# Decoder block with routed experts: the fourth round of token numbers moved ahead of the first expert

## The reference

```
logits = xf @ Wr + br                       # 2048 tokens, 8 experts
G, idx = top_k(softmax(logits).T, 256)      # each expert takes its 256 best tokens
tokens = xf[idx]
mid = silu(tokens @ W_up[expert // 2] + b_up)      # 256 -> 682
out = mid @ W_down[expert] + b_down                # 682 -> 256
y = zeros.at[idx].add(G * out)
```

## Time and profile before

| | us |
|---|---|
| median of 3 runs | 308.36 (307.84 to 310.17) |
| profiled execution | 308.39 |
| its span in the profile | 306.6 |
| busy: PE / PEld / DVE / ACT / POOL | 252.1 / 204.8 / 195.3 / 154.6 / 144.2 |

### The profile page before, as it was taken

One profiled execution on the slowest core, in us unless ns is written; L12 is line 12 of the kernel. 1 busy time (PEld: TensorE's weight loads), 2 busy tenths in 40 slices (PEclk: granted clock), 3 DMA queues, 4 the chain that ended last, 5 costly groups with the idle time before them and its releaser, 6 DMA issues.

```text
span 306.6 us, 5179 instructions
## 1 busy us (share of the span) xinstructions
PE 252.1 (82%) x1699; PEld 204.8 (67%) x1699; DVE 195.3 (64%) x590; ACT 154.6 (50%) x322; POOL 144.2 (47%) x212
## 2 busy tenths in 40 slices
PE   8998999899988999999995111377499999999790
PEld 4754557666555879989883011246399999999790
DVE  1644467277967578767776787841437775776484
ACT  4643302635497555555223576403237987875124
POOL 6806923715444312535578459277372244443033
PEclk9999999999999999999999555557689999999997
DMA  6960021017092818320000999733045846522637
GB/s 193 294 118 14 1 62 45 0 36 169 6 209 67 198 40 188 71 53 0 3 1 5 282 356 385 250 90 106 19 87 135 214 70 121 123 32 32 156 141 271
DMA packets 33403, 35.59 MB, mean 116 GB/s; under 512 B 10338, under 2 KB 25698, under 8 KB 33122
## 3 DMA queue, kind: packets, MB, share of 16 engines
q1 hardware_dynamic: 30002, 31.16, 35.9%
q0 software_dynamic: 2784, 4.00, 7.8%
q10 hardware_dynamic: 592, 0.12, 0.2%
HBM read 18.16 MB, written 8.19 MB: 86 GB/s over the span
## 4 chain that ended last, share of the span: by engine, by line
PE 58%; DVE 14%; ACT 10%; DMA 6%; issue 5%; POOL 3%; another core or an unknown queue 1%; SPq 1%; DVEq 0%; POOLq 0%; ACTq 0%
PE bank L1163 13%; PE bank L1400 8%; PE bank L1611 6%; PE bank L1351 4%; PE bank L1249 3%; PE bank L1320 2%; DVE junk L1962 2%; PE bank L1387 2%; DMA WUR<-in_L_ffn_W_up 2%; DMA Y<-summed_rows 2%; ACT bank L1107 2%; PE bank L1334 2%; POOL rstd L787 1%; PE bank L1258 1%
## 5 line engine op out<-in xcount | busy, mean ns | idle before, releaser
L786 POOL TENSOR_SCALAR var_eps<-mean_var 128x1 f32<-128x1 f32 (+2 forms) x37 | 8.4, 226 | 75.3 <-DVE mean_var L1806 74.7
L858 POOL DMA_INDIRECT summed_rows<-OUT,idx x14 | 21.7, 1549 | 36.6 <-DVE OUT L2080 34.5
L1400 PEld LDWEIGHTS bank<-VB,PT 128*128 128x128 f32 x256 | 32.4, 192 | 1.5
L1400 PE MATMUL bank<-VB,PT 128*128 128x34 f32 x256 | 31.0, 268 | 0.0
L1163 PE MATMUL bank<-FTH,WUH 128*128 128x256 f32 x94 | 28.4, 303 | 2.6 <-DVE idx L2056 2.6
L1107 ACT ACTIVATE bank<-bank,b_up_c 128x256 f32<-128x256 f32 (+1 forms) x48 | 19.4, 446 | 17.1 <-PE bank L1163 15.4
L1163 PE MATMUL bank<-FTL,WUH 128*128 128x256 f32 x94 | 27.7, 295 | 0.0
L1163 PE MATMUL bank<-FTH,WUL 128*128 128x256 f32 x94 | 27.7, 295 | 0.0
L1813 DVE TENSOR_REDUCE NMF<-bank 128x8 f32<-128x512 f32 x32 | 21.7, 680 | 6.8 <-PE bank L1363 6.7
L1611 PE MATMUL bank<-WDH,MH 128*128 128x256 f32 x80 | 23.7, 296 | 1.2 <-DVE ML L2094 1.2
L848 POOL DMA_INDIRECT XG<-routed_rows,idx x16 | 17.0, 1061 | 15.6 <-DVE idx L2056 11.3
(11 more groups left out here) (339 smaller groups left out, 744.7 us busy)
## 6 DMA issues: line engine op xcount, KB each, us to landing
WDR<-in_L_ffn_W_down SPq DMA_DIRECT2D x8, 640.0 KB
QS<-QH SPq DMA_DIRECT2D x32, 128.0 KB, 3.0
WUR<-in_L_ffn_W_up SPq DMA_DIRECT2D x4, 682.0 KB, 4.7
routed_rows<-X SPq DMA_DIRECT2D x2, 1056.0 KB, 10.2
X<-in_x SPq DMA_DIRECT2D x4, 512.0 KB, 5.1
QS<-QL SPq DMA_DIRECT2D x16, 128.0 KB, 3.0
summed_rows<-X SPq DMA_DIRECT2D x2, 1024.0 KB, 9.9
Y<-summed_rows SPq DMA_DIRECT2D x8, 256.0 KB, 5.4
```

The source lines that it names most:

```text
L858: pool.indirect_dma_start(summed, bass.IndirectOffsetOnAxis(ap=idx[:, 2 * e + h:2 * e + h + 1].bitcast(U32), axis=0), OUT[:, (2 * e + h) % ...
L1400: last = pe.matmul(o[:, j * 34:(j + 1) * 34], PT[m % 2][:, j, s * P:(s + 1) * P], VB[:, m // 2, j].rearrange("p h d -> p (h d)"), start=Tr ...
```

## The change

The whole of round 3 goes to the end of the other rounds, on PE and on DVE. On PE `slot_numbers(3)` stands before the wait for "st" and the unread product, `row_numbers(3)` behind it; of the four unread products one is left. On DVE `one_hots(3)` goes between `numbered(2)` and `by_slot(2)`, and `numbered(3)` between `by_slot(2)` and `by_row(2)`. Nothing of it is left in the loop over the expert steps. The computation is the same.

```diff
--- before.py
+++ after.py
@@ -1545,13 +1545,13 @@
             slot_numbers(0)
             row_numbers(0)
             slot_numbers(1)
+            row_numbers(1)
+            slot_numbers(2)
+            row_numbers(2)
+            slot_numbers(3)
             wait_moved(pe, "st")
             keep_busy(0, 1)
-            row_numbers(1)
-            keep_busy(0, 2)
-            slot_numbers(2)
-            keep_busy(0, 1)
-            row_numbers(2)
+            row_numbers(3)
 
             def tokens(e):
                 if e == 0:
@@ -1616,10 +1616,6 @@
 
             for kind, *at in expert_steps:
                 {"gt": tokens, "up": up, "dn": down}[kind](*at)
-                if (kind, *at) == ("up", 0, 1):
-                    slot_numbers(PAIRS - 1)
-                if (kind, *at) == ("up", 0, 2):
-                    row_numbers(PAIRS - 1)
 
             pe.wait_ge(rows_made, 2)
             for h in range(2):
@@ -2066,8 +2062,12 @@
             one_hots(2)
             by_row(1)
             numbered(2)
+            one_hots(3)
             by_slot(2)
+            numbered(3)
             by_row(2)
+            by_slot(3)
+            by_row(3)
 
             dve.wait_ge(stack_masks, 1)
 
@@ -2115,15 +2115,8 @@
                     at = slice(P if e == 0 else 0, TOP)
                     dve.tensor_tensor(FTL[:, e % 4, :, at], got[:, :, at], FTH[:, e % 4, :, at].bitcast(F32),
                                       ALU.subtract).then_inc(sem_moved(step), 1)
-                if step == ("up", 0, 0):
-                    one_hots(PAIRS - 1)
-                    numbered(PAIRS - 1)
                 if step[0] == "up":
                     middle_low(*step[1:])
-                    if step == ("up", 0, 1):
-                        by_slot(PAIRS - 1)
-                    if step == ("up", 0, 2):
-                        by_row(PAIRS - 1)
                     if step[2] == 1 and LOW_BY_DVE <= e + 1 < E:
                         down_low(e + 1)
                     if step[2] == 2 and e % GS == 0 and e // GS + 1 < NG:
```

## The result

| | before | after |
|---|---|---|
| median of six runs, us | 307.92 (307.75 to 310.17) | 312.10 (310.89 to 314.52) |
| ratio (95% interval) | | 1.0131 (1.0103 to 1.0159) |
| profiled execution, us (its span) | 308.39 (306.6) | 313.83 (312.0) |
| busy PE / DVE / ACT / POOL, us | 252.1 / 195.3 / 154.6 / 144.2 | 250.8 / 195.6 / 154.7 / 143.2 |

The kernel is slower by 4.2 us, on the other side of no change from the forecast of 300.3 and outside its range of 299 to 307. PE works 1.3 us less and the time is longer all the same. Some executions of each of these kernels take several us more at a lower granted clock; the ratios leave them out.

What follows compares the result with a forecast made beforehand. PE was taken to set the experts' pace, broken by one hole with an unnamed 4.29 us stall. Earlier up(1,0) (-5.9) and the kept clock (-2.2) gave -8.1 us: 308.4 to 300.3 us, range 299 to 307.

Steps and rivals of the forecast that it cites:

- What bounds the kernel: PE paces the experts, except a hole at 213.0 to 219.4 us with a 4.29 us unnamed wait and a clock fall.
- (a): Three of four unread PE products go; they stood in waits for DVE, so nothing is subtracted.
- (b): Round 3 before the experts: tokens(0) 0.75 us late, hidden by the second gather; 0.75 us at most if cover fails.
- (c): POOL's wait for idx of round 3 goes, worth 0; the second gather beside OHT3 costs 0.2 us.
- rival C: In expert 0 the stall lasts until the gathers end: release 221.1, up(1,0) 222.5, half-speed loss stays, 311.5 us; chance 0.06.
- (d): First expert without round 3: up(1,0) at 213.5 instead of 219.38, 5.9 us saved, if the stall goes with slot_numbers(3).
- (e): PE's hole behind expert 0 shrinks from 6.6 to about 1.3 us, so the clock stays up: 2.2 us saved.
- Rival D: The clock's rise at 210.8 is missed and comes at 217.6, costing 3.0 us: 303.3 us; chance 0.08.

Runs made afterwards that it cites:

- e12: Kernel before with one unread product in place of four, round 3 still inside expert 0: 308.88 us, 1.0007.
- e17: e9 with the third and fourth gather issued only once idx of round 3 is made: 299.66 us, 0.9719.
- e2: Kernel after with POOL's pause put back, the last four gathers waiting for ML of up(0,2): 308.17 us, 1.0017.
- e9: Kernel after, gathers in short early runs: four, four more after FTL of expert 1, then pairs three experts ahead: 301.54 us, 0.9773.
- e15: Kernel after with a POOL fill before each gather from the fifth on, one every 2.25 us or more: 307.37 us, 0.9942.
- e5: Kernel after with four gathers, then a pair for expert e + 2 behind the copies of expert e + 1: 308.74 us, 1.0023.
- e11: Kernel after without its last unread product: 309.32 us, 1.0.
- e14: Kernel after without its last unread product, again, on the same chip as e13: 310.68 us, 1.0056.
- e3: Kernel before with the gathers from the fifth on waiting for FTL of expert 1: 313.72 us, 1.0199.
- e6: e5 plus twelve unread gathers of 96-byte rows in one run behind the first four: 320.18 us, 1.0397.
- e1: Kernel after with the gathers from the fifth on waiting for FTL of expert 1: 307.38 us, 0.998.
- e13: Kernel after unaltered, compared again on another chip: 311.49 us, 1.0076.
- e16: Kernel after with one POOL pause, behind the eighth gather until FTL of expert 1: 303.57 us, 0.986.
- e18: e9 unaltered, run again on the same chip as e17: 301.22 us, 0.9772.
- e7: e5 plus twelve unread plain 135 KB transfers from SP beside the dense products of expert 0: 309.40 us, 1.0023.

## Why the prediction was wrong, point by point

**What bounds the kernel: right.** The unnamed wait was found and named as the thing everything depends on. That PE's completions come out late there was right as well.

**(a) Fillers worth 0: right.** e12, 1.0007 (0.9978 to 1.0036).

**(b) Round 3 before the experts: the schedule right, the cover broken.** Without late completions it runs as laid out: in e17 idx3 is at 203.02 (forecast 203.0) and up(0,0) starts at 204.70 (forecast 204.7 to 204.9). In the kernel after, slot_numbers(3) stands beside the third gather and its release is 1.5 us late, so idx3 is at 205.04, tokens(0) at 204.90 and up(0,0) at 207.10, 2.4 us behind the earlier trace rows, of which 0.25 came from ahead of this stage (first gather at 199.17 against 198.92). The clock's first rise came later too: 213 - (0.68 - 0.5)/0.5 x 2 = 212.3 us instead of 210.8. The forecast added 0.2 us for this part and bounded it at 0.75 if the cover fails; it measured 2.2.

**(c) Gathers "worth 0": this is the step that failed.** Its question was who waits for the last four gathers, and the answer, nobody, was right. What it did not count is what POOL's 5.3 us wait for idx did for the others: it ended the run of gathers, and the held completions came out 1.9 us later. The change took that wait away, the run went from twelve to sixteen, and the release from 216.15 to 221.40, as in rival C (221.1). e2 puts the pause back and the loss is gone. In the sum the place of this 0 was taken by the lost pause: up(1,0) moved by +4.8 us instead of -5.9. The price for the second gather beside OHT3 was right: 1.14 against 0.96 us, 0.18 for the 0.2 taken. It is not the price of every such product: the gather at 204.25 in the kernel before took 0.95 us beside OHL and OHH of round 3 (204.79, 205.13).

**(d) up(1,0) at 213.5: wrong in the kernel after (224.22), right where no long close run stands beside expert 0** (213.65 in e9, 213.24 in e15, 213.01 in e17; 215.07 in e5, where expert 0 began later). The arithmetic held; the assumption "the stall goes with slot_numbers(3)" did not. The reason for it was that the stall began inside or behind slot_numbers(3). That was where a wait first showed it; whether completions were late before it, the trace cannot show, except that the SiLU of up(0,1) still started promptly at 210.40.

**(e) The clock: right for a short hole, but the hole did not shrink.** With the hole down to 1.0 us it stayed at 1.00 (e9, e15), and so the 2.2 us would have come. With the hole longer it fell again, and PE ran at half speed from 224.22 to 229.4, 5.1 us, as before (5.1 us): the term measured 0, as rival C said. Rival D did not come: the first rise was 1.5 us late, not missed.

**Rival C** gave 311.5 us and was given 0.06; measured 312.10. Its mechanism is right; that its number is so near is partly luck. It let the release free FTH(1), and up(1,0) start 1.4 us later, at 222.5. In fact the SiLU of up(0,1) was held too, and four operations, itself among them, stand between the release and up(1,0): 2.8 us, 224.22. The profiled execution, 313.83, carries this; in the median execution the hold may have been shorter, as it was in e11 and e14. That up(0,1) ended 2.4 us later by (b) is the likely reason that its SiLU was caught, and no run separates it. The argument against the gathers was "gathers ran from 202 on as well, and ACT followed PE at once": true of the first ones in that kernel, and e3 and e6 show long holds only later in a run. One number, the 1.9 us of the earlier trace rows, spoke for C and was put down as a coincidence. For the forecast's own assumption only the place of the stall spoke, so the two deserved chances nearer to each other.

**The total.** 300.3 us was the price of a kernel without holds, and e17, the same change with no more than four gathers in a row, takes 299.66. The agreement is not a proof of the sum, since POOL's order is another in all of the expert stage of e17.

## What to carry to other kernels

Before a wait is taken off a queue that "nobody waits for", ask what its pause did for the others: here it ended a run of indirect gathers. Where an engine waits for PE microseconds longer than PE's records last, look for POOL's indirect transfers in the same stretch, and issue them in runs of at most four, or some 2.2 us apart, with each pair early enough for its reader. These two figures are those of e9, e17 and e15. An unnamed release is not to be credited to the instruction that happens to stand beside it; of two guesses at its cause, the one that a distance in the trace repeats deserves the larger chance.

## What the runs showed of the hardware

- Completions of PE, as ACT and DVE see them, come out late while POOL issues indirect gathers every 1.25 us: up to 8.9 us behind the end of PE's record in the kernel after. In the same stretch DVE follows ACT at once (MH ends at 212.90, ML starts at 212.93).
- Long holds came only in runs of twelve and more: the longest single wait was 2.9 us (e12), 4.3 us (before, e2), 5.9 us (e1) and 7.9 us (e3) with twelve, 8.5 us (after), 7.0 us (e13), 4.0 us (e14) and 3.5 us (e11) with sixteen. Runs of eight left 1.1 us (e16). The third and fourth gather of a run already held lh of round 3 by 1.4 us (e18), yet not ACT's copies beside the same gathers in the kernel before (202.84, 204.04).
- It does not depend on the bytes (96 or 1056 a row), plain transfers of SP do not cause it even with the DMA engines busy to 0.90 (e7), and 2.25 us between gathers end it (e15).
- PE's own products pause too near the end of a run that goes over into scatters, by up to 1.03 us (e1) and 1.71 us (e3), with no wait shown.
- Runs that mix four gathers, two scatters and two gathers, with 0.3 us between them (e9, from 213.86 on), show no hold. A scatter's issue takes 1.6 us against 0.95, so the mean distance is longer there; whether that or the number of gathers counts, no run tells.
- Open: what inside the chip is shared between the two, whether "indirect" or "issued by POOL" is what matters, and why some completions come out in the middle of a run (e3, e6, e11, e14) and others 2 to 4.5 us behind it. A run of the same length with nothing computed by PE beside it was not tried.
